# Diagonal tiles in three steps, without early queries times late keys in the value products

## The reference

```python
c_Q = x @ W_DQ.T;  q = concat([(c_Q @ W_UQ.T), rope(c_Q @ W_QR.T)])       # per head, 128 + 64
c_KV = x @ W_DKV.T;  k = concat([(c_KV @ W_UK.T), rope(x @ W_KR.T)])      # the rotary part is shared
scores = clip(q . k, -80, 80);  scores = where(pos_q >= pos_k, scores, -inf)
weights = softmax(scores / sqrt(192));  attn = weights @ (c_KV @ W_UV.T)
s = attn.reshape(S, 2048) @ W_O.T
out = x + s * silu(x @ weight.T + lora experts with a top-2 router)
```

## Time and profile before

| | us |
|---|---|
| median of 3 runs | 1422.66 |
| lowest, highest | 1422.1, 1424.13 |
| the profiled execution | 1422.12 |
| its span, first to last instruction | 1420.6 |

### The profile page before, as it was taken

One profiled execution on the slowest core, in us unless ns is written; L12 is line 12 of the kernel. 1 busy time (PEld: TensorE's weight loads), 2 busy tenths in 40 slices (PEclk: granted clock), 3 DMA queues, 4 the chain that ended last, 5 costly groups with the idle time before them and its releaser, 6 DMA issues.

```text
span 1420.6 us, 27596 instructions
## 1 busy us (share of the span) xinstructions
PE 1379.9 (97%) x9810; PEld 1142.2 (80%) x9810; DVE 1148.5 (81%) x1339; ACT 783.3 (55%) x861; POOL 125.0 (9%) x175
## 2 busy tenths in 40 slices
PE   7999689999999999999999999999999999999998
PEld 6888568788778887888888888788788699978887
DVE  7666378888898898989889898898788878967665
ACT  4232367666666666666666665666656756533221
POOL 0000112101101101010010100111100011021220
PEclk9999899999999999999999999999999999999999
DMA  7332665545425333324142332444422133165552
GB/s 291 118 101 84 178 199 160 166 133 155 124 85 159 93 121 77 128 80 132 55 129 85 101 113 55 123 154 134 134 57 61 67 116 114 47 206 171 172 156 89
DMA packets 110769, 174.91 MB, mean 123 GB/s; under 512 B 9608, under 2 KB 65160, under 8 KB 108168
## 3 DMA queue, kind: packets, MB, share of 16 engines
q1 hardware_dynamic: 93880, 108.99, 24.6%
q0 software_dynamic: 16016, 63.80, 15.5%
q10 hardware_dynamic: 832, 1.57, 0.5%
HBM read 125.83 MB, written 48.50 MB: 123 GB/s over the span
## 4 chain that ended last, share of the span: by engine, by line
PE 78%; DMA 5%; DVE 5%; ACT 2%; issue 0%; SPq 0%; ACTq 0%
PE score_ps L1187 30%; PE out_ps L1209 19%; DMA key_slot<-keys 5%; PE score_ps L1303 4%; PE score_ps L1302 4%; PE score_ps L1304 4%; PE out_ps L1228 2%; PE out_ps L1229 2%; PE out_ps L1232 2%; PE score_ps L1157 1%; PE score_ps L1158 1%; PE score_ps L1160 1%; PE score_ps L1159 1%; DVE prob_l L1499 1%; DVE prob L1486 1%; PE score_ps L1122 1%
## 5 line engine op out<-in xcount | busy, mean ns | idle before, releaser
L1362 ACT CAST prob_h<-prob 128x1024 fp32r<-128x1024 f32 (+1 forms) x288 | 290.4, 1008 | 232.4 <-DVE prob L1481 184.8
L1187 PE MATMUL score_ps<-q_h,key_slot 64*128 64x512 f32 x1792 | 363.7, 392 | 6.1 <-DMA key_slot<-keys 6.0
L1499 DVE TENSOR_TENSOR prob_l<-prob,prob_h 128x1024 fp32r<-128x1024 f32 (+1 forms) x288 | 336.0, 1167 | 39.8 <-ACT prob_h L1362 38.3
L1356 ACT ACTIVATE prob<-score_ps 128x1024 f32<-128x1024 f32 (+1 forms) x288 | 282.2, 980 | 152.6 <-PE score_ps L1187 103.0
L1209 PE MATMUL out_ps<-prob_h,value_slot 64*128 64x512 f32 (+1 forms) x1792 | 345.2, 375 | 0.0
L1494 DVE TENSOR_TENSOR total<-total,prob 128x1024 f32<-128x1024 f32 (+1 forms) x256 | 295.0, 1152 | 0.0
L1481 DVE TENSOR_SCALAR prob<-prob 128x1024 f32<-128x1024 f32 x224 | 155.2, 693 | 72.7 <-ACT prob L1356 72.6
L1187 PEld LDWEIGHTS score_ps<-q_h,key_slot 64*128 64x128 f32 x1792 | 177.2, 184 | 41.1 <-issue 10.3
L1209 PEld LDWEIGHTS out_ps<-prob_h,value_slot 64*128 64x128 f32 x1792 | 177.2, 184 | 31.6 <-DVE prob_l L1499 2.1
L1187 PE MATMUL score_ps<-q_l,key_slot 64*128 64x512 f32 x896 | 180.6, 390 | 0.0
L1187 PE MATMUL score_ps<-rot_hh,key_slot 64*128 64x512 f32 x896 | 180.4, 389 | 0.0
(11 more groups left out here) (210 smaller groups left out, 2005.5 us busy)
## 6 DMA issues: line engine op xcount, KB each, us to landing
key_slot<-keys SPq DMA_DIRECT2D x144, 256.0 KB, 2.7
value_slot<-values SPq DMA_DIRECT2D x144, 128.0 KB, 2.0
rot_hh<-turned POOLq DMA_DIRECT2D x30, 512.0 KB, 6.2
heads_rows<-head_rows POOLq DMA_DIRECT2D x15, 1024.0 KB, 9.7
turned<-rot_hl POOLq DMA_DIRECT2D x14, 1024.0 KB, 4.6
rows<-heads_rows SPq DMA_DIRECT2D x28, 512.0 KB, 5.8
rot_l<-turned POOLq DMA_DIRECT2D x30, 256.0 KB, 7.7
x_in<-in_x SPq DMA_DIRECT2D x16, 256.0 KB, 2.6
```

The costliest lines, as they stand in the source:

```text
L1187: mm = pe.matmul(score_ps[:, half, c * 512:(c + 1) * 512], keys_of[ROWS[r], :], moving[par][ROWS[r], half * HW + c * 512:half * HW + (c + ...
L1356: nc.scalar.activation(prob[half][:, 0:width], score_ps[:, half, 0:width], ACT.Exp, scale=QK_SCALE).then_inc(exp_done, 1)
L1362: nc.scalar.copy(prob_h[half][:, 0:width], prob[half][:, 0:width]).then_inc(high_done, 1)
L1499: nc.vector.tensor_tensor(p_l, p, p_h, ALU.subtract).then_inc(split, 1)
```

## The change

Columns: a unit's 2,048 columns are ordered (half, query tile, head, token of 128) instead of (half, head, token of 256), so that one query tile's 512 columns of a half lie together.

Steps: the first query tile's diagonal (768 columns: 512 "late" ones, tokens 64 to 127 of 8 heads, and 256 "early" ones), the rectangle (second query tile against key tile 2m, 1,024 columns, no mask), the second query tile's diagonal (768 columns). Early queries see only the first 64 keys; the early columns of heads 0 to 3 are put on partitions 0 to 63 and those of heads 4 to 7 on partitions 64 to 127, with a shifted copy of the keys between zeros (`early_keys`). In the value products the late columns use all rows (two halves of 256 columns), the early ones 64-row couples with a second copy of the first 64 value rows (`value_early`). The value products of the rectangle and of the second diagonal tile run in the first full step.

Loads: a third key buffer holds the diagonal's keys, so those of full steps 0 and 1 are loaded during the corner; early keys (4 x 64 columns) and early values (64 rows) are loaded besides. The turned queries lie in HBM as the gather wants them: it reads rot_hh in rows of 8 KB, and each store of turned queries becomes 8 DMAs of 128 KB from 32 partitions.

```diff
-            sp.dma_start(turned_out[n].rearrange("w p n -> p w n"),
-                         raw(rot_hl[n]).rearrange("p w e n -> p w (e n)")).then_inc(turned_stored, 16)
+            for home, source in turned_parts(turned_out[n], rot_hl[n]):
+                sp.dma_start(home, source).then_inc(turned_stored, 16)
...
+def turned_parts(unit, rot_hl):
+    halves = raw(rot_hl).rearrange("p w e (c x) -> p w e c x", c=2)
+    for q in range(4):
+        for w in range(2):
+            home = unit[w].rearrange("f e (h c q x) -> f e h c q x", h=2, c=2, q=2)[:, :, q // 2, :, q % 2, :]
+            yield home, halves[q * HALF:(q + 1) * HALF, w, :, :, :]
...
-        self.causal = sb("causal", [P, CT], F32)
+        self.causal = sb("causal", [P, 2, DQ], F32)
+        self.sides = sb("sides", [P, 2], F32)
...
-        key_slot = [sb(f"key_slot{n}", [P, SK], F32R) for n in range(2)]
+        key_slot = [key_even, key_odd, sb("key_slot2", [P, SK], F32R)]
+        value_early = sb("value_early", [P, SV], F32R)
+        early_keys = sb("early_keys", [P, 4, 3 * DQ], F32R)
...
+                if kind == CORNER:
+                    load_keys(t, k, DIAGONAL)
+                    load_early_keys(unit, k, kind)
+                    sp.wait_ge(scored, 2 * (t - 1))
+                    load_keys(t + 1, 0, 0)
...
+                    sp.wait_ge(scored, 2 * t)
+                    load_keys(t + 2, 1, 1)
+                    load_values(t, k, slot)
+                    load_early(t, unit, k, kind, prev)
...
+            def late_scores(unit, par, slot, c, buffer):
+                for n, (keys_of, moving) in enumerate(blocks):
+                    pe.matmul(score_ps[:, buffer, 0:512], keys_of, tile_of(moving[par][:, :], c)[:, :, :, DQ:P],
+                              start=n == 0, stop=n == len(blocks) - 1)
+                pe.wait_ge(early_keys_in, 16 * (2 * unit + c + 1))
+                for n, (_, moving) in enumerate(blocks):
+                    for half in range(2):
+                        mm = pe.matmul(score_ps[:, buffer, 512:DW], early_keys[:, block_of[n], (1 - half) * DQ:(1 - half) * DQ + P],
+                                       tile_of(moving[par][:, :], c)[:, half, :, 0:DQ],
+                                       start=n + half == 0, stop=n + half == len(blocks))
...
+            def weigh_late(t, n, slot, buffer, c, last):
+                for half in range(2):
+                    for step, (word, weights) in enumerate(passes):
+                        pe.matmul(bank(half)[:, :, DQ:P], value_slot[slot][:, word:word + P],
+                                  heads(weights[buffer][:, half * 256:(half + 1) * 256]),
+                                  start=step == 0 and c == 0, stop=False)
+                for word, weights in passes:
+                    for half, (rows, values_of) in enumerate(zip(ROWS, (value_slot[slot], value_early))):
+                        mm = pe.matmul(bank(half)[:, :, 0:DQ], values_of[rows, word:word + P],
+                                       heads(weights[buffer][rows, 512:DW]), start=False, stop=last and word == P)
...
                 if kind == FULL:
...
                         for crossed in (False, True):
-                            half_scores(full, half, par, slot, crossed)
-                            half_weigh(full, t - 1, half, 1 - slot, prev, crossed)
+                            half_scores(full, half, par, keys_of, buffer, crossed)
+                            if prev == FULL:
+                                half_weigh(full - 2, t - 1, half, 1 - slot, buffer, crossed)
+                            elif not crossed and half == 0:
+                                weigh_second(t - 2, slot, buffer, n if unit.has_second else None)
+                            elif not crossed:
+                                weigh_late(t - 1, n, 1 - slot, buffer, 1, False)
```

555 lines of the change are left out of this document (346 added, 209 removed).

## The result

The changed kernel is slower: 1457.28 us (median of 4, 1453.6 to 1460.0) against 1422.82, a ratio of 1.0235 (95% interval 1.0223 to 1.0247), 32 to 35 us. The forecast was 1430, with 1446 as its upper end. The profiled execution took 1458.29 us, its span 1456.8 (before: 1420.6).

A forecast was written before the change was run, and what follows sets the result against it. TensorE's queue, busy 97% of the span, was taken as the bound. The terms -8.7 + 16.5 - 4.6 + 3 + 1.5 = +7.7 on the profiled 1422.1 us gave 1429.8, as a median 1430 us; range 1416 to 1446.

The forecast's parts named there:

- Slots: TensorE's matmul slots in the 14 units with full steps: 45 instead of 48 a unit, -8.7 us.
- Switches: Changes between 64-row and 128-row matmuls on TensorE: 6 more in each of 14 units at 0.197 us, +16.5 us.
- the rival that they are free: Changes of tile shape on TensorE cost nothing, so 1413 us; chance 0.14 for free or half price.
- Key waits: TensorE's ten waits for key tiles vanish, -7.6 us at most; VectorE takes 0.3 back in each: -4.6 us.
- End of the first stage: SP's 2 stores of turned queries become 16, so the next stage starts later: +3 us (0 to +5.2).
- Units 0 to 2: Second stage's first units hang on gathers; POOL's store in 8 pieces signals later: +1.5 us (-1 to +4).
- Gathers: Reading rot_hh in one 8 KB piece instead of four of 2 KB gains nothing: 0 (bounds -2 and 0).
- Small loads: 32 new loads each of early keys and early values on SP's queue: 0 (bounds 0 and +4).
- Addresses: Left-side buffers land 32 B past a multiple of 64, odd units slow down: 1439 us, up to 1446; chance 0.22.
- Waits in the new chain: The single late step delays the first full steps, up to 0.6 us in 14 units: 1438 us; chance 0.12.

The follow-up runs named there:

- the two queues: Changed kernel with the second eight stores of turned queries at the first stage's end issued by POOL beside SP's first eight: 1450.92 us, 1.0209.
- the fastest kernel: Kernel before with its key load ahead of the value loads and the two turned-query additions moved to either side of the first clip: 1418.13 us, 0.9969.
- the repeat: Changed kernel run again unedited, to know its scatter: 1454.41 us, 1.0229 against the kernel before.

## Why the prediction was wrong

*Slots, -8.7 us: right in the count.* Unit 10 has 371 slots instead of 374 ("Saved 0.62 us"); no run changes them alone.

*Switches, +16.5: right.* Eight a unit at the measured distances; the rival that they are free is refuted in each of the units. With slots this gives 0.56 us a unit; units 5 to 13 cost 0.72. The Trainium skill (TensorEngine Tiling (Array Packing), Key Properties) says that a change of tiling mode drains the engine; the trace agrees that a change costs. A row of 64-row matmuls also pays, 0.33 us, where a crossed group follows a straight one with nothing between and waits for its semaphore.

*Key waits, -4.6: wrong by about 7.* The step "VectorE ... I take 0.3 back in each of ten" set the next-late work from one even unit, as if it were the engine's pace. What followed in each unit was a fixed queue: clip behind two additions, copy behind clip, split behind copy. It gives back all that a shorter wait gives. Its price is 0.72 - 0.56 = 0.16 us a unit on top instead of 0.33 gained. Removing most of the key waits alone, on the kernel before, gave no measurable gain (0.9994); moving the two additions as well, 4.4 us.

*End of the first stage, +3 (0 to 5.2): too small.* 5.9 us (the table's other 0.6 lie ahead of the stores). The direction was right. Of it 3.3 are the pieces and 2.6 the layout. The layout's part is the issues': 16 times 0.68 instead of 0.50 us are 2.9. The term's upper end was itself summed too low: it gave the four stores behind the sixteen 1.3 us, where the earlier trace rows has 2.53. The middle of the forecast, which let issues and transfers overlap, was too hopeful: with one queue the issues set the end, and the two queues show that the transfers allow nothing sooner.

*Units 0 to 2, +1.5 (-1 to +4): the step that failed.* 17 to 21 us, against 1.5 forecast, more than half of the whole error. I wrote "the slots and switches of units 0 and 1 count nothing" and costed only POOL's store. But the change also moves the last unit's late value product behind the second scores, hence ScalarE's copy of the head rows behind its second copy of probabilities, and the sums, the latent queries and the gather behind that. None of these were on my list, as the list was made by stretches with full steps and the first units have none. Shown by one run: the latent queries ahead of the sums give 7.4 us of it back. The stores in pieces are 2.7 by the run on the kernel before. The rest, 7 to 11 us, is read from the traces and no edit removed it: unit 2's key tile that lands 3 us after the gather; the half clock, which costs about 5 us in unit 2 and differs by 3 us in unit 1 between two executions of the same kernel; and about 1 us before unit 0, where early keys load among the first gather's data (its last part takes 10.5 us instead of 9.3; that they cause it is not shown). These overlap with the 7.4 and are not a sum.

*Gathers, 0: right.* In the first wait the DMA share is 1.04 at 195 GB/s with one piece a row; with four it was 1.07 at 223. Unit 2's gather takes 9.7 us instead of 9.9. The Trainium skill (SBUF — State Buffer, Door 1: The DMA port swizzle) says that 64 adjacent partitions reach only half of the 16 ports; the traces agree: before, the stores from 128 partitions ran at 418 GB/s at a share of 1.02 (142 to 144 us), and contiguity gave nothing on 64.

*Small loads, 0 (0 to +4): right from unit 5 on.* In units 3 and 4 TensorE waits twice for a value tile (2.2 us, above), whose load lands with the burst of gather and head rows; no run tells what part of this the new loads have. The Trainium skill (DMA: Bandwidth & Descriptors, Specifications) wants 512 B a piece for line rate; the profile's page of the changed kernel agrees, where 128 KB in pieces of 256 B land no sooner than 256 KB of key tiles (one that had the queues nearly to itself, at 174.50, took 2.74 us):

```profile
key_slot<-keys SPq DMA_DIRECT2D x144, 256.0 KB, 2.7
...
early_keys<-keys SPq DMA_DIRECT2D x32, 128.0 KB, 3.2
```

*Rivals.* Addresses: refuted, odd units keep their pace (0.227 us a slot). Waits in the new chain: there are none in front of the late tile's product; the waits came two steps later. The true mechanism, a longer chain behind the units without full steps, was no rival of mine.

## What to carry to other kernels

When a change reorders products inside a loop, list for each operation that moves what other engines read from it, and follow that chain in the iterations with the least work (the first, the last), not in the typical one: there nothing hides it. When a wait is removed, look at the in-order queue of the engine that is late next for work that could stand elsewhere; on the kernel before, moving two additions of 0.69 us gave 2.8 us over nine units, where removing most of the wait had given 0.1. And a matmul group that must follow another on the same banks wants something between the two; work moved out of that place is paid for there (0.33 us here).

## What the runs showed of the hardware that was not expected

A 256 KB load issued inside a burst of 2.5 MB (gather and head rows) lands with the burst's end, after 10.6 us (issued at 207.5) or 7.3 us (issued at 210.7), instead of 2.7. The granted clock did not follow the length of the idle time ahead of it alone. It was 0.50 behind idle times of 4.46 and 3.15 us (after, unit 1), 3.57 and 3.20 us (POOL's store in pieces), 2.92 us (SP's stores in pieces, 206.8) and 2.01 us (the fastest kernel, 201.4); it stayed at 1.00 behind 1.77 and 2.30 us (before) and behind 3.15 us in the repeat (201.3). Two profiled executions of one kernel thus differ by 3.1 us in unit 1, while nine of the later units agree to 0.3 us.
